# A Mamba-style decoder block on one core: one section of outputs and transposes per tile step, the decays' differences on GpSimd

## What is computed

```python
proj = einsum('bsd,ed->bse', x, in_proj_w)       # 8192 gate, 8192+1024+1024 hBC, 128 dt
hBC = silu(conv_4_taps(hBC) + conv_b)            # hs: 128 heads of 64; B, C: 8 groups of 128
dt = clip(softplus(dt + dt_bias), 0, 100)
A_cum = cumsum(dt * -exp(A_log))                 # along the 128 tokens of a sequence
L = where(l >= s, exp(A_cum[l] - A_cum[s]), 0)   # per head
Y = einsum('C[l,n] B[s,n] L[l,s] (hs*dt)[s,p]') + hs * D
g = Y * silu(gate)
out = group_rms_norm(g) * norm_w                 # 8 groups of 1024 channels
x = layernorm(x + einsum('bsi,oi->bso', out, out_proj_w))
```

## Time and profile before

| | before |
|---|---|
| median of 3 runs | 1743.92 us (1743.9 to 1744.66) |
| profiled execution | 1743.17 us, span 1741.5 us |
| PE busy | 1659.1 us (95%) |
| DVE busy | 1196.1 us (69%) |
| ACT busy | 1103.3 us (63%) |
| POOL busy | 710.6 us (41%) |
| mean granted TensorE clock | 0.988 of 2.4 GHz |

### The profile page before, as it was taken

One profiled execution on the slowest core, in us unless ns is written; L12 is line 12 of the kernel. 1 busy time (PEld: TensorE's weight loads), 2 busy tenths in 40 slices (PEclk: granted clock), 3 DMA queues, 4 the chain that ended last, 5 costly groups with the idle time before them and its releaser, 6 DMA issues.

```text
span 1741.5 us, 26304 instructions
## 1 busy us (share of the span) xinstructions
PE 1659.1 (95%) x9160; PEld 1275.5 (73%) x9160; DVE 1196.1 (69%) x2257; ACT 1103.3 (63%) x2352; POOL 710.6 (41%) x588
## 2 busy tenths in 40 slices
PE   6899999999999999999999999999999987889998
PEld 4777787778777877787778777877787765444656
DVE  4775758675867586758685868586858676896443
ACT  3675668575847594759474948494849482996231
POOL 3363536352626263626361636164616352331000
PEclk8999999999999999999999999999999988999999
DMA  5232213221323131313131313131413273001000
GB/s 200 70 113 73 97 63 120 73 97 55 122 78 98 49 121 64 118 43 128 55 127 43 127 54 128 43 122 48 140 34 115 65 104 111 1 1 37 13 13 24
DMA packets 76551, 138.88 MB, mean 80 GB/s; under 512 B 6786, under 2 KB 13954, under 8 KB 76164
## 3 DMA queue, kind: packets, MB, share of 16 engines
q1 hardware_dynamic: 76420, 137.21, 24.9%
HBM read 134.55 MB, written 2.63 MB: 79 GB/s over the span
## 4 chain that ended last, share of the span: by engine, by line
PE 44%; DVE 33%; ACT 15%; issue 6%; DMA 1%; SPq 1%; POOL 0%; DVEq 0%; ACTq 0%
DVE conv L729 13%; PE ps_hs L1093 6%; PE ps_hs L1095 6%; PE ps_hs L1094 6%; ACT ps_dec L531 6%; DVE xdt L753 4%; DVE m_sb L762 4%; ACT L531 3%; ACT sq_tmp L541 3%; PE ps_hs L246 3%; PE ps_y L1320 3%; PE ps_hs L1282 3%; PE ps_dec L1282 3%; PE ps_hs L248 3%; PE ps_hs L247 3%
## 5 line engine op out<-in xcount | busy, mean ns | idle before, releaser
L378 POOL TENSOR_SCALAR_AFFINE_SELECT cum_bc<-cum_bc 128x1024 f32<-128x1024 f32 x128 | 141.4, 1105 | 501.5 <-DMA cum_bc<-cum_scratch 501.5
L729 DVE SCALAR_TENSOR_TENSOR conv<-ps_hs,cw,conv 128x508 f32<-128x508 f32 (+2 forms) x432 | 319.6, 740 | 36.8 <-ACT conv L495 26.6
L531 ACT ACTIVATE ps_dec<-cum_bc,neg_cum 128x128 f32<-128x128 f32 x1024 | 308.8, 357 | 0.8
L762 DVE TENSOR_TENSOR m_sb<-ps_dec,cb 128x512 f32<-128x512 f32 x256 | 169.6, 686 | 154.6 <-ACT ps_dec L531 154.6
L246 PE MATMUL ps_hs<-x_hi,w_hi 128*128 128x512 f32 x576 | 231.9, 403 | 15.6 <-DVE conv L729 7.6
L246 PE MATMUL ps_gate<-x_hi,w_hi 128*128 128x512 f32 x576 | 239.5, 416 | 0.0
L495 ACT ACTIVATE conv<-ps_hs,cbias,cw 128x512 f32<-128x512 f32 x144 | 110.6, 769 | 189.5 <-PE ps_hs L248 189.5
L248 PE MATMUL ps_gate<-x_hi,w_lo 128*128 128x512 f32 x576 | 226.3, 393 | 0.0
L1093 PE MATMUL ps_hs<-wo_hi,g_hi 128*128 128x512 f32 x512 | 204.4, 399 | 22.8 <-DVE acc L889 8.4
L247 PE MATMUL ps_hs<-x_lo,w_hi 128*128 128x512 f32 x576 | 225.6, 392 | 0.0
L248 PE MATMUL ps_hs<-x_hi,w_lo 128*128 128x512 f32 x576 | 225.6, 392 | 0.0
(11 more groups left out here) (141 smaller groups left out, 3092.8 us busy)
## 6 DMA issues: line engine op xcount, KB each, us to landing
cum_bc<-cum_scratch SPq DMA_DIRECT2D x128, 512.0 KB, 4.0
w_raw<-w_in SPq DMA_DIRECT2D x145, 256.0 KB, 4.6
wo_raw<-w_out SPq DMA_DIRECT2D x64, 256.0 KB, 4.9
g_acc<-x_t SPq DMA_DIRECT2D x4, 512.0 KB, 6.8
acc<-x_nat SPq DMA_DIRECT2D x1, 2048.0 KB, 9.4
k_rep<-ctx_t SPq DMA_DIRECT2D x8, 256.0 KB, 12.6
out<-y_out SPq DMA_DIRECT2D x8, 256.0 KB, 2.0
wg_sb<-w_gate SPq DMA_DIRECT2D x1, 1792.0 KB, 12.4
```

The costliest lines, as they stand in the source:

```text
L531: x = sc.activation(ps_dec[e][:, cols], cum_bc[bh][:, e, cols], ACT.Exp, bias=neg_cum[:, bh * HB + b, head:head + 1])
L729: v.scalar_tensor_tensor(out=dst, in0=src, scalar=cw[:, at, TAPS - 1 - n:TAPS - n], in1=dst, op0=ALU.mult, op1=ALU.add).then_inc(S["tap"], 1)
L762: v.tensor_tensor(flat(m_sb[:, q]), ps_dec[q % 2][:, :], flat(half(cb, q // 2)), ALU.mult)\
```

## The change

Per tile step PE now has one section that isn't projections: outputs(0), outputs(1), then the transposes of the **next** tile, both halves, into `ps_gate` in place of `ps_y`. `gates` therefore waits for `scale_dt` and the transposes for the silu of the gates. `ps_y` belongs to the outputs alone, and `combine`, `squares`, `g_low` and `add_square` of tile t move into the next step. The 192 products of a half group stand behind the projections of the next step (`group_products`), ahead of that step's outputs. `cb_products` and the square sums come behind them in the B and C step. In ACT each `decay` is one exponential of 512 columns without a bias: POOL adds the negated cumulated decays to the masked `cum_bc` (`differences`, 128 x 1024, 128 in all) with a broadcast operand. With the last tile, PE does 12 of its half group's products before the outputs.

```diff
-                                 pattern=[[0, 2 * HB], [1, SEQ]], channel_multiplier=-1).then_inc(S["bc_ok"], 1)
+                                 pattern=[[0, 2 * HB], [1, SEQ]], channel_multiplier=-1).then_inc(S["causal"], 1)
+
+            def differences(t, bh):
+
+                if t == 0:
+                    pool.wait_ge(S["neg_cum_ok"], bh + 1)
+                pool.wait_ge(S["causal"], 2 * t + bh + 1)
+                part = cum_bc[bh][:, :, :].rearrange("p e (b s) -> p e b s", s=SEQ)
+                start = half(neg_cum, bh)[:, :, 2 * t:2 * t + 2].rearrange("p b e -> p e b").unsqueeze(3)
+                gp.tensor_tensor(part, part, start.broadcast_to([P, 2, HB, SEQ]), ALU.add).then_inc(S["bc_ok"], 1)
...
+                if s == 0:
+                    differences(0, 0)
+                    differences(0, 1)
                 if holds_bc(s):
+                    if s:
+                        add_square(tile_at(s - 1), 0)
+                        add_square(tile_at(s - 1), 1)
                     continue
                 t = tile_at(s)
                 j = t % TPH
-                if j:
+                if t % TPG:
+                    add_square(t - 1, 0)
                     add_square(t - 1, 1)
                 if t + 1 < TILES:
-                    keep_causal(t + 1, 0)
-                    keep_causal(t + 1, 1)
+                    for bh in range(2):
+                        keep_causal(t + 1, bh)
+                        differences(t + 1, bh)
                 if j == 0 and t:
                     wait_alone(pool, S["o_ps"], BATCH * (t // TPH))
...
-                add_square(t, 0)
-                if j == TPH - 1:
-                    add_square(t, 1)
+            add_square(TILES - 1, 0)
+            add_square(TILES - 1, 1)
...
             def decay(t, q):
 
                 bh, e = q // 2, q % 2
-                if t == 0 and e == 0:
-                    act.wait_ge(S["neg_cum_ok"], bh + 1)
                 if e == 0:
                     act.wait_ge(S["bc_ok"], 2 * t + bh + 1)
+                if t % TPG == 0 and bh == 0:
+                    act.wait_ge(S["cb_sb"], 2 * (t // TPG) + e + 1)
                 need(act, S["m_ok"], 4 * t + q - 1)
-                head = 2 * t + e
-                for b in range(HB):
-                    cols = slice(b * SEQ, (b + 1) * SEQ)
-                    x = sc.activation(ps_dec[e][:, cols], cum_bc[bh][:, e, cols], ACT.Exp,
-                                      bias=neg_cum[:, bh * HB + b, head:head + 1])
-                x.then_inc(S["exp_ok"], 1)
+                sc.activation(ps_dec[e][:, :], cum_bc[bh][:, e, :], ACT.Exp).then_inc(S["exp_ok"], 1)
...
             for s in range(STEPS):
                 more = s + 1 < STEPS
                 if holds_bc(s):
                     if s:
-                        root_group(s // PER - 1)
+                        squares(tile_at(s - 1), 0)
                     first_tap(s + 1, 0, 0)
+                    if s:
+                        squares(tile_at(s - 1), 1)
                     first_tap(s + 1, 0, 1)
                     for h in range(2):
                         silu(s + 1, 0, h)
                         gate(s + 1, h)
                     continue
                 t = tile_at(s)
-                j = t % TPH
+                inner = t % TPG > 0
+                if t and not inner:
+                    root_group(t // TPG - 1)
                 decay(t, 0)
                 decay(t, 1)
-                if j:
-                    squares(t - 1, 1)
+                if inner:
+                    squares(t - 1, 0)
+                decay(t, 2)
                 if more:
                     first_tap(s + 1, 0, 0)
-                decay(t, 2)
+                if inner:
+                    squares(t - 1, 1)
                 decay(t, 3)
...
+                if not more:
+                    scale_out(t)
+                    continue
+                first_tap(s + 1, 0, 1)
+                silu(s + 1, 0, 0)
...
+                silu(s + 1, 0, 1)
+                scale_out(t)
...
+            squares(TILES - 1, 0)
+            squares(TILES - 1, 1)
...
-                    ps_y[r][:, :].rearrange("p (b e d) -> p b e d", b=HB, e=2),
+                    ps_gate[r][:, :].rearrange("p (b e d) -> p b e d", b=HB, e=2),
...
+            for s in range(STEPS):
+                more = s + 1 < STEPS
+                if holds_bc(s):
+                    g = s // PER
+                    t = tile_at(s - 1)
+                    if s:
+                        combine(t, 0)
+                        combine(t, 1)
+                    taps(s + 1, 0, 0)
+                    if s:
+                        g_low(t, 0)
+                        taps(s + 1, 0, 1)
+                        g_low(t, 1)
+                        keep_products(t)
+                        dve.wait_ge(S["ss_ps"], g)
+                        v.tensor_scalar(rstd_g[:, :], ps_y[0][:, 0:BATCH], 1.0 / (TPG * P), EPS, ALU.mult, ALU.add)\
+                            .then_inc(S["rstd_v"], 1)
+                    keep_cb(g, 0)
+                    keep_cb(g, 1)
...
+                        taps(s + 1, 0, 1)
+                    continue
+                t = tile_at(s)
+                inner = t % TPG > 0
+                if inner:
+                    combine(t - 1, 0)
+                    combine(t - 1, 1)
+                else:
+                    dve.wait_ge(S["cb_sb"], 2 * (t // TPG) + 2)
+                decay(t, 0)
+                scale_dt(t, 0)
+                scale_dt(t, 1)
+                decay(t, 1)
+                if more:
+                    taps(s + 1, 0, 0)
+                decay(t, 2)
+                if more:
+                    taps(s + 1, 0, 1)
+                decay(t, 3)
+                if inner:
+                    g_low(t - 1, 0)
+                    g_low(t - 1, 1)
+                if more and holds_bc(s + 1):
+                    taps(s + 1, 1, 0)
+                    taps(s + 1, 1, 1)
+                if inner and t % TPH == 0:
+                    keep_products(t - 1)
+
+            combine(TILES - 1, 0)
+            combine(TILES - 1, 1)
+            g_low(TILES - 1, 0)
+            g_low(TILES - 1, 1)
...
-                else:
-                    pe.wait_ge(S["sg_ok"], 2 * tile_at(s) + h + 1)
+                elif h == 0:
+                    pe.wait_ge(S["xdt_ok"], 2 * tile_at(s) + 2)
...
-            def transposes(s, r):
+            def transposes(s):
 
                 t = tile_at(s)
-                pe.wait_ge(S["silu_ok"], conv_at(s) + r + 1)
-                need(pe, S["g_lo_ok"], 2 * t + r - 1)
-                for b in range(HB):
-                    mm = pe.transpose(ps_y[r][:, b * P:(b + 1) * P], hs[s % 2][:, r * HB + b, :], ident[:, :])
-                mm.then_inc(S["tr_ok"], 1)
+                pe.wait_ge(S["silu_ok"], conv_at(s) + 2)
+                pe.wait_ge(S["sg_ok"], 2 * t + 2)
+                for r in range(2):
+                    for b in range(HB):
+                        mm = pe.transpose(ps_gate[r][:, b * P:(b + 1) * P], hs[s % 2][:, r * HB + b, :], ident[:, :])
+                    mm.then_inc(S["tr_ok"], 1)
 
             def outputs(t, bh):
 
                 pe.wait_ge(S["m_ok"], 4 * t + 2 * bh + 2)
-                pe.wait_ge(S["xdt_ok"], 2 * t + bh + 1)
+                if bh == 0:
+                    pe.wait_ge(S["xdt_ok"], 2 * t + 2)
+                    need(pe, S["g_lo_ok"], 2 * t)
...
+            def group_products(t, early):
+
+                done = BATCH * (t // TPH)
+                pe.wait_ge(S["wo_lo_ok"], t + 1)
+                for b in range(2):
+                    for n in range(early, TPH - 1):
+                        out_products(b, n)
+                for b in range(BATCH):
+                    if b % HB == 0:
+                        pe.wait_ge(S["g_lo_ok"], 2 * t + 1 + b // HB)
+                    if b == 0 and t == TILES - 1:
+                        square_sums(t)
+                    if b >= 2:
+                        pe.wait_ge(S["gacc_ok"], done + b - 1)
+                        for n in range(TPH - 1):
+                            out_products(b, n)
+                    out_products(b, TPH - 1).then_inc(S["o_ps"], 1)
...
             for s in range(STEPS):
                 more = s + 1 < STEPS
+                t = tile_at(s)
                 if more:
                     pe.wait_ge(S["w_lo_ok"], s + 2)
                     free_hs(s)
-                if holds_bc(s):
-                    need(pe, S["gacc_ok"], 2 * BATCH * (s // PER))
+                    kept = t if holds_bc(s) or t % TPG == 0 else t - 1
+                    need(pe, S["gacc_ok"], BATCH * (kept // TPH))
                     heads(s + 1, 0)
                     heads(s + 1, 1)
...
+                if holds_bc(s):
+                    if s:
+                        free_hs(s + 1)
+                        group_products(tile_at(s - 1), 0)
+                        square_sums(tile_at(s - 1))
```

(37 more changed lines are left out.)

113 lines of the change are left out of this document (22 added, 91 removed).

## The result

The changed kernel takes **1689.39 us** (median of 4 runs, 1687.67 to 1692.2) against 1743.91 of the kernel before in the same job: ratio 0.9689, interval 0.9673 to 0.9706. Forecast were 1699, a range of 1688 to 1732, and 1690 to 1710 for the likeliest case alone, whose edge this just misses.

A forecast was written before the change was run, and what follows sets the result against it. PE's instruction stream was taken as the bound. Terms -22.4, -27, -1 and +2.5 gave -48 us; with 3 us added for thin margins, -45, hence 1699 us against 1743.9, range 1688 to 1732.

The forecast's parts named there:

- the false lead: DVE's 154.6 us of waiting for ACT's exponentials: the place to gain only if DVE set the pace, which it doesn't.
- Term 1: PE's inner step: one section with outputs instead of two, 64 times 0.35 us, -22.4 us.
- -22.4 if the transposes add nothing: Bound on the section saving: -22.4 us if transposes behind outputs add nothing, -10 if each kind costs its own 0.2.
- the hole moves along: Rival: outputs behind projections and transposes behind outputs cost as much as the two sections; only waits go; 1721 us, chance 0.1.
- Term 2: PE's waits in and around the products: 3.8 of 4.8 us per full group gone, -27 us, bounds 0 and -34.
- ACT's relief: Four wide exponentials per tile for sixteen: ACT sheds 2.5 us per tile, is off the path, worth 0 to the time.
- the ring: Outputs, combine, DVE's step, g_low, next outputs: closes with 0.4 us to spare; as rival bound 1723 us, chance 0.2.
- Tail -1: After the last gates: outputs(62, 0), about 1.2 us, move under cover of SP's transfers, -1 us.
- Start +2.5: Kernel start: transposes wait for ACT's gate, first differences stand behind POOL's split; next gates near 68.8, not 67.1; +2.5 us.
- The 3 us allowance: Added to the sum because the thin margins (ring, masks, table loads) won't all hold: about 0.1 us in half the steps.
- the steps 3 and 7: Tile steps of a group whose differences would be the place where POOL becomes the bound.
- this rival: POOL becomes the bound, kernel slower: 1776 us at 3.4 us per difference, deciding from 3.3 on; chance 0.08.

The follow-up runs named there:

- experiment 1: Changed kernel with the old decays: 1702.35 us; kernel before, in its old order, with differences on POOL and four 512-column exponentials per tile: 1730.83 us.
- experiment 3: Changed kernel with two sections of outputs, each followed by its half's transposes: 1705.53 us; with half 0's transposes ahead of one section instead: 1689.88 us.
- experiment 2: Changed kernel with products directly behind their half group's last outputs, as before the change: 1734.9 us; the same with the old decays: 1737.13 us.
- experiment 5: Changed kernel with mask and v_raw transfers ahead of k_rep's: 1681.22 us; also with negation behind the last sums and each first_part directly before its second_part: 1681.93 us.
- the run at 2.5: Changed kernel with only half 1's mask done twice on POOL, 1.10 us more per tile: 1692.13 us.
- experiment 4: Changed kernel with extra work per tile: second scale_dt done twice, 1699.09 us; both masks twice on POOL, 1719.74 us; only half 1's mask twice, 1692.13 us.
- experiment 6: Changed kernel plus 15 POOL additions of 128 x 376 in five operand forms; mostly 0.98 to 1.05 us each, 0.81 with a broadcast operand; no kernel time given.

## Why the prediction was right, and where it was not

**What bounds the kernel.** Right: PE's stream. DVE's 154.6 us were the false lead the prediction called them: 63 of them gone alone is worth 12.7 (experiment 1).

**Term 1, one section instead of two, -22.4.** The mechanism is right, the size too small: the inner step fell by 0.45, not 0.35, so 64 x 0.45 = 28.8. The prediction found 0.77 us in the old step above the bare instructions (13.53), gave 0.35 to each section and left 0.07 standing. The new step is 13.85 - 13.53 = 0.32 above them: the remaining section costs about what it did, and 0.10 more went with the other. Of the old step's seven changes of kind, four were entries into and exits from outputs; the new one has three in all, two of them such. To which change the further 0.10 belonged the runs don't say. "-22.4 if the transposes add nothing" was no bound, since they could also save. That transposes behind outputs cost nothing of their own is shown (experiment 3), and with it the rival "the hole moves along" is out. The Trainium skill (TensorE: Matmul & The Clock Gate, Step-by-step: what each phase is for) says that PE pulls weight loads ahead of matmuls in flight. The trace agrees among the projections, where a load starts 0.22 us ahead of its matmul, and not on the way into and out of the 64-column outputs, where it starts only with it (experiment 3).

**Term 2, the waits, -27.** Per full group 3.3 us went, not 3.8: 2.2 in the first half's products, 0.1 in the second's, 0.5 at the last outputs of each half (1.49 and 1.51 us in the old trace, 1.02 in its other steps). 7 x 3.3 = 23. From the account: the loop's 54.2, less 28.8, less 1.2 for the outputs that now stand behind the last gates, is 24.2. The size is right within 3 us. But its cause isn't the new place alone: in experiment 1 the short exponentials took 10.0 us of such waits away in the old place, and with the old exponentials in the new place the products run as in the changed kernel. Either does a good part of the work. And its description was wrong: as "waits that the place removes", independent of term 1. In the new order the products at their old place cost +45 (experiment 2); the place is what term 1 rests on. Nothing in the prediction asked what the old place would cost in the new order.

**ACT's relief, "worth 0".** Wrong by 13 us, in the old order and in the new (experiment 1). Its working was right, 2.4 us per tile shed and ACT off the path on average; but the ring it named two lines above, with 0.4 us to spare, runs through ACT's exponentials. A term costed at nothing because of an average has to be held against the thinnest wait that passes through it. The total wasn't hurt, since the relief was in the measured order anyway.

**Tail -1, measured -3.9:** 1.2 for the moved outputs, as said, and 2.7 from the last gates on. The chain of SP was the right one (experiment 5); it was faster here, with 8.85 us to issue k_rep where it took 9.65. Nine other kernels with this tail took 9.2 to 9.8 and resumed 28.1 to 31.4 us after the last gates, so the 2.7 are luck of the profiled execution. **Start +2.5, measured +1.5:** the differences of tile 0 ran at 56.67, before the next split, since POOL had been waiting there 12.62 us for neg_cum. The prediction had put them behind the split that ended at 63.2, which is now the one after them. The transposes did wait for ACT's gate (1.66), but the next gates started at 67.07, not 68.8: the wait for scale_dt that made up most of the term didn't come.

**The 3 us allowance** wasn't spent: inner steps of 13.85 throughout, group after group 169.6. The misses add up: 3 (allowance) + 6.4 (term 1) - 2.8 (term 2) + 2.9 (tail) + 1.0 (start) = 10.5, from 1698.2 to 1687.67. That the forecast of 1699 came within 10 us of the median 1689.39 owes something to two misses of opposite sign, 6.4 and -2.8. The range's low end was also added up a little low: its own terms give 1689, with which the median is inside by 0.4 us.

**The margins.** The ring: 0.4 us predicted, 0.42 measured. POOL: the prediction had the whole gain lost from 3.3 us per difference on, by its two points (3 us per half there, 5 at 3.4) so steeply that nothing would be lost below 3.15. Measured: nothing to be told at 2.5, 30 us at 3.04, so the loss begins earlier. Carried on in a straight line the gain of 54 would be gone near 3.5, and 3.4 would give some 1738, not 1776; that is an estimate from two points, with an onset somewhere between them, and nothing beyond 3.04 was tried. The place was nearly right: the fourth and the eighth tile of a group are the steps 3 and 7 that it named, though what is late there are the differences made one step earlier. What decided against this rival was the price: 1.94 us, where 2.4 was taken and 2.1 to 2.5 named as the sign of being right. The lower end came from k_bd, a row with a broadcast operand, too, but in pieces of 512 columns. At 2.4 nothing to speak of would have been lost either, by the run at 2.5. The lower price is also why POOL is busy for 947 us in all, not the 1020 forecast.

**The rule on engine choice.** The Trainium skill (GPSIMD Engine Reference, section 4.1, Engine selection) says that an elementwise add belongs on VectorE, as GpSimd is about twice as slow with two inputs. By the rows POOL takes 1.94 us where DVE would take some 1.4 (two additions of 512 columns at 0.69), a ratio of 1.4 for this form; and POOL's time was free while it stayed within its margin (experiment 4).

## What to carry to other kernels

An operation that another engine waits for has a price even when the engine is off the path on average: look for the shortest ring that passes through it and count what is to spare there, per step, for every engine in it. When two sections of a pipeline are merged, ask in the same breath which later work now lacks cover; here, with the old decays, the merge alone was worth 7 us and the merge with the moved products 41. Order the transfers behind a freed buffer by who waits first: that gave 8 us for two moved lines. And before a few microseconds of one profile are credited to a change, look at the same stretch in the traces of the other kernels: the tail here scattered by 3 us with its transfers unchanged.

## What the runs showed of the hardware that was not expected

- A TensorE wait of 2.5 us is followed by a granted clock of 0.55 and 0.59 for some 4 us (1.2 GHz for most of it), and costs 1.4 us more than itself. In that kernel three waits of 2.5 to 2.7 us are followed by such a stretch, four of 2.3 to 2.4 are not; in the kernel with the masks doubled one of 2.1 us is.
- On POOL a two-input addition is 0.8 of its usual time when one operand is broadcast along the columns: 1.94 against 2.41 us for 1024 columns, 0.81 against 0.99 for 376.
- The first weight load of a section of 64-column outputs, and the first behind it, start only with their own matmuls, where among projections a load starts 0.22 us ahead.
- Operations of DVE and POOL that lie in SBUF alone slow each other. Two sums of DVE took 2.76 us with k_bd beside them, 2.09 with a copy of POOL beside part of them, and one takes 0.72 alone; that pair of k_bd took 2.48, and 2.04 without the sums beside it. In experiment 6 POOL's addition went from 0.81 to 1.14 and DVE's from 0.69 to 0.98.
